# Eight-head attention layers: softmax sums done in one go in a bank of the shared ring, their accumulator's bank used as a third score bank

## What is computed

```
xn  = group_norm(x) * gn_w + gn_b
qkv = qkv_w @ xn + qkv_b                      # per head: q, k, v of 32 x 1024
w   = softmax(einsum('bct,bcs->bts', q * scale, k * scale))
a   = einsum('bts,bcs->bct', w, v)
out = (xn or x) + proj_w @ a + proj_b         # xn in layer 2, x in layer 3
```

## Time and profile before

| | us |
|---|---|
| median of 3 runs | 1897.23 |
| the profiled execution | 1903.71 |
| its span, first to last instruction | 1901.6 |

### The profile page before, as it was taken

The page is one execution under the profiler, slowest core; times in us unless marked ns, Lnnn a source line. Parts: engine busy times, 40 slices in busy tenths (PEclk is TensorE's granted clock), DMA queues, the critical chain, the costliest instruction groups (busy, mean ns, idle before and its releaser), DMA issues.

```text
span 1901.6 us, 24881 instructions
## 1 busy us (share of the span) xinstructions
PE 1707.0 (90%) x8222; PEld 1007.7 (53%) x8222; DVE 1099.5 (58%) x1571; ACT 928.7 (49%) x1487; POOL 1010.4 (53%) x402
## 2 busy tenths in 40 slices
PE   3887959999992899999999998999999999999987
PEld 2666748888882454454444444445444444454422
DVE  2545535454432856765766667666675576666712
ACT  2433414343322165655565564565665656555553
POOL 2322312122103166775787585767776578757764
PEclk7989979999996698999999998999999999999988
DMA  3000000000001222021130230202202112032000
GB/s 137 17 17 17 1 1 1 1 1 1 1 1 32 56 68 67 1 68 45 25 67 1 67 84 1 67 20 54 67 2 67 42 49 67 2 90 68 1 23 22
DMA packets 24989, 67.44 MB, mean 35 GB/s; under 512 B 7200, under 2 KB 8992, under 8 KB 24864
## 3 DMA queue, kind: packets, MB, share of 16 engines
q1 hardware_dynamic: 24864, 65.78, 14.3%
HBM read 7.82 MB, written 4.19 MB: 6 GB/s over the span
## 4 chain that ended last, share of the span: by engine, by line
PE 50%; DVE 9%; issue 3%; ACT 3%; POOL 1%; DMA 1%; SPq 1%; DVEq 0%; POOLq 0%; ACTq 0%
PE psO L869 13%; PE psA L950 12%; PE psD L925 11%; PE psD L79 10%; DVE A L979 5%; PE psO L872 4%; DVE BNS L998 4%; ACT PR L1121 2%; POOL PA L1187 1%; DMA QS<-MROW 1%; SPq L1207 0%; ACT XH L1065 0%; SPq L1209 0%; DVE A L981 0%; DMA QS<-SL 0%
## 5 line engine op out<-in xcount | busy, mean ns | idle before, releaser
L1121 ACT ACTIVATE PR<-psA 128x512 f32<-128x512 f32 x1024 | 585.0, 597 | 520.3 <-PE psA L950 491.3
L998 DVE TENSOR_REDUCE BNS<-psD 128x1 f32<-128x512 f32 x1024 | 632.6, 685 | 241.5 <-PE psD L925 241.4
L1187 POOL TENSOR_TENSOR PA<-PA,PR 128x2048 f32<-128x2048 f32 x128 | 585.1, 4571 | 20.5 <-ACT PR L1121 9.3
L950 PE MATMUL psA<-QS,KS 97*128 97x512 f32 x1024 | 463.5, 461 | 39.1 <-ACT PR L1121 30.5
L925 PE MATMUL psD<-KS,QS 96*128 96x512 f32 x1024 | 419.2, 446 | 33.2 <-DVE BNS L998 17.8
L950 PEld LDWEIGHTS psA<-QS,KS 97*128 97x128 f32 x1024 | 194.2, 193 | 335.0 <-ACT PR L1121 180.0
L869 PE MATMUL psO<-PR,V 128*32 128x512 f32 x2048 | 273.3, 642 | 0.7 <-ACT PR L1121 0.7
L925 PEld LDWEIGHTS psD<-KS,QS 96*128 96x128 f32 x1024 | 204.2, 200 | 123.9 <-DVE BNS L998 80.2
L594 POOL TENSOR_SCALAR P<-P,RS 128x1024 f32<-128x1024 f32 x64 | 71.8, 1122 | 356.1 <-DVE RS L345 356.1
L1187 POOL TENSOR_TENSOR PA<-PR 128x2048 f32<-128x2048 f32 x32 | 146.0, 4564 | 134.9 <-ACT PR L1121 134.9
L979 DVE RECIPROCAL A<-psO 128x512 f32<-128x512 f32 x32 | 107.4, 3358 | 148.0 <-PE psO L872 148.0
(11 more groups left out here) (129 smaller groups left out, 1810.7 us busy)
## 6 DMA issues: line engine op xcount, KB each, us to landing
KS<-SH SPq DMA_DIRECT2D x128, 128.0 KB, 2.5
QS<-SH SPq DMA_DIRECT2D x128, 128.0 KB, 2.5
KS<-SL SPq DMA_DIRECT2D x64, 128.0 KB, 2.5
QS<-SL SPq DMA_DIRECT2D x64, 128.0 KB, 2.5
X<-x SPq DMA_DIRECT2D x4, 1024.0 KB, 7.6
out<-X SPq DMA_DIRECT2D x4, 1024.0 KB, 4.4
KH<-KL SPq DMA_DIRECT2D x8, 128.0 KB, 2.3
QH<-KL SPq DMA_DIRECT2D x8, 128.0 KB, 2.4
```

What stands on the lines that cost most here:

```text
L950: e.matmul(psA[:, s % 2, :], KS[0:STACK + 1, p, q, j * PART:(j + 1) * PART], QS[0:STACK + 1, p, q, h * HALF:(h + 1) * HALF], start=True, s ...
L998: top = e.tensor_reduce(MXH[:, h, q, tile:tile + 1], full, AX.X, ALU.max)
L1121: e.activation(PR[:, J % 4, (s % QUADH) * HALF:(s % QUADH + 1) * HALF], psA[:, s % 2, :], ACT.Exp, scale=scale).then_inc(exp_done, 1)
L1187: e.tensor_tensor(PA[:, :], PR[:, (J - 1) % 4, :] if j == 1 else PA[:, :], PR[:, J % 4, :], ALU.add).then_inc(sum_done, 1)
```

## The change

`psO` bank 1 no longer holds the sums. It becomes a third bank for scores (`score_bank`), and score s waits for exp s-3 instead of s-2; only scores 0 and 1 of a phase with P even still wait for s-2. The three sum pieces of a half are a new side unit "z" in the ring of `psD`: `sums` does sum 7, sum 6 and pa one after the other, at 34.9 (step 35) for half 0 and at 2.9 (step 3) of the next phase for half 1. DVE's `take_half` is z's taker: its reciprocal reads the ring's bank and then frees it. av 6 and 7 are both issued at step 33 of the half (so those of half 1 at step 1 of the next phase; before, av 6 was at step 62). The m units begin at 6.5 instead of 5.5, the hole for the reciprocal is 35 to 38.5 in all phases (before 35 to 39, and one more at 12 to 13.5 in phases with P even). `av_done` counts 7 pieces a half instead of 8, and the waits on it follow. POOL's first add of a half waits for z instead of pa. In `tail` the last z and the output projection use ring banks in turn.

```diff
-        M_AT = (5.5, 58)
-        HOLES = [[(35, 39)], [(12, 13.5), (35, 39)]]
+        M_AT = (6.5, 58)
+        HOLES = [(35, 38.5)]
...
+                     "z": (34.9, 2.9)}
         BANKS = 4
+        SCORE_BANKS = 3
...
+        def score_bank(s, p):
+
+            i = (s + p) % SCORE_BANKS
+            return psA[:, i, :] if i < 2 else psO[:, 1, :]
...
-        WEIGH = [("av", 0, 13), ("av", 1, 13), ("av", 2, 18), ("av", 3, 18), ("av", 4, 26), ("av", 5, 26),
-                 ("av", 6, 30), ("sum", 6, 30), ("av", 7, 34), ("sum", 7, 34), ("pa", NT, 35)]
...
+        WEIGH = [(0, 13), (1, 13), (2, 18), (3, 18), (4, 26), (5, 26), (6, 33), (7, 33)]
+        PIECES = NT - 1
+
+        def weighed(P, J):
+
+            h, j = J // NT, J % NT
+            return PIECES * 2 * P + PIECES * h + min(j + 1, PIECES)
...
+                    def sums(full, P, h):
+
+                        for j in (NT - 1, NT - 2, NT):
+                            if j == NT:
+                                wait(e, sum_done, ADDS * (2 * P + h + 1))
+                            source = PA[:, :] if j == NT else PR[:, j % 4, :]
+                            source = source.rearrange("p (q n) -> p q n", q=QUADH)
+                            for q in range(QUADH):
+                                mm = e.matmul(full[CH * q:CH * q + CH, :], ones[:, 0:CH], source[:, q, :],
+                                              start=(j == NT - 1), stop=(j == NT))
+                            if j == NT - 2:
+                                mm.then_inc(av_done, 1)
+                        return mm
...
+                        elif u == "z":
+                            mm = sums(full, P - i, i)
...
-                            wait(e, exp_done, STEPS * P + s - 1)
-                            e.matmul(psA[:, s % 2, :], KS[0:STACK + 1, p, q, j * PART:(j + 1) * PART],
+                            wait(e, exp_done, STEPS * P + s - (1 if p == 0 and s < 2 else SCORE_BANKS - 1))
+                            e.matmul(score_bank(s, p), KS[0:STACK + 1, p, q, j * PART:(j + 1) * PART],
...
-                        for i in range(2 * CT):
-                            e.wait_ge(vec_free, TAIL["vector"] - BANKS + 1 + i)
-                            output(bank(4, i), i, 2 * NGRP, 3).then_inc(d_full, 1)
+                        e.wait_ge(vec_free, TAIL["vector"] + 1)
+                        sums(bank(4, 2), NGRP - 1, 1).then_inc(d_full, 1)
+                        for i in range(2 * CT):
+                            e.wait_ge(vec_free, TAIL["vector"] + max(i, 2))
+                            output(bank(4, 3 + i), i, 2 * NGRP, 3).then_inc(d_full, 1)
...
-                    def take_half(P, p, h):
-
-                        wait(e, av_done, (2 * P + h + 1) * NT)
+                    def take_half(full, p, h):
+
                         out_ap = A[:, p, h * HALF:(h + 1) * HALF]
-                        e.reciprocal(out_ap, psO[:, 1, :])
+                        e.reciprocal(out_ap, full).then_inc(vec_free, 1)
                         e.drain()
                         e.tensor_tensor(out_ap, psO[:, 0, :], out_ap, ALU.mult).then_inc(out_done, 1)
```

More of the change, by code:

```diff
@@ L698, in side_units @@
             units = [(u, at, i) for u, ats in halves.items() for i, at in enumerate(ats)]
+            if first:
+                units = [x for x in units if x[0] != "z" or g == 1 and x[2] == 0]
             n = QUADH * NT * 2
-            spacing = (M_AT[1] - M_AT[0] - sum(b - a for a, b in HOLES[g])) / n
+            spacing = (M_AT[1] - M_AT[0] - sum(b - a for a, b in HOLES)) / n
             for i in range(n):
                 at = M_AT[0] + i * spacing
-                for a, b in HOLES[g]:
+                for a, b in HOLES:
                     at += (b - a) * (at > a)
@@ L726, in attention_stack @@
         assert LOOP["all"] % BANKS == 0
-        assert all("".join(x[0] for x in u[-BANKS:]) == "m" * (BANKS - 1) + "T" for u in UNITS)
+        assert all("".join(x[0] for x in u[-BANKS:]) == "m" * (BANKS - 1) + "T" for u in UNITS[:4])
         def base_of(kind, place, r):
+            if place == 4:
+                return TAIL[kind]
             return BASE[kind][place] if r is None else r * LOOP[kind] + BASE[kind][place]
@@ L988, in add_residual, with take @@
                                                       in1=xb, op0=ALU.add, op1=ALU.add)
-                    def take(place, r, k, G, g, proj, layers):
+                    def take(place, r, k, p, G, g, proj, layers):
                         u, _, i = UNITS[place][k]
@@ L1020, in phase @@
                     def phase(P, p, G, g, place, r, layers, proj=None, norm=None, norm_b=None):
-                        events = [(at, 0, k, "unit") for k, (u, at, i) in enumerate([] if G is None else UNITS[place])
+                        events = [(at, 0, k, "unit") for k, (u, at, i) in enumerate(UNITS[place])
                                   if u not in "vwkqKQ"]
@@ L1026, in phase @@
                             events.append((XN_AT + 0.1, 0, 0, "weights"))
-                        if P is not None:
-                            if not (isinstance(P, int) and P == 0):
-                                events.append((TAKE_AT - HALF_STEPS, 0, 1, "half before"))
-                            events.append((TAKE_AT, 0, 0, "half"))
                         for _, _, k, what in sorted(events):
-                            if what == "half before":
-                                take_half(P - 1, 1 - p, 1)
-                            elif what == "half":
-                                take_half(P, p, 0)
-                            elif what == "weights":
+                            if what == "weights":
                                 split_next_weights()
@@ L1090, in phase @@
                         events = []
-                        for k, (u, at, i) in enumerate([] if G is None else UNITS[place]):
+                        for k, (u, at, i) in enumerate(UNITS[place]):
                             if u in "vwkqKQ":
@@ L1182, in phase @@
                                 wait(e, exp_done, STEPS * P + QUADH * (J + 1))
-                                if j == 1:
-                                    wait(e, av_done, NT * (2 * P + h))
-                                else:
+                                if j == 1 and not (isinstance(P, int) and P == h == 0):
+                                    before = [k for k, (u, _, i) in enumerate(UNITS[place]) if u == "z" and i == 1 - h][0]
+                                    e.wait_ge(d_full, base_of("all", place, r) + before + 1)
+                                if j > 1:
                                     wait(e, sum_done, ADDS * (2 * P + h) + j - 1)
```

67 lines of the change are left out of this document (29 added, 38 removed).

## The result

| | before | after |
|---|---|---|
| median of 20 runs each, us | 1901.47 (1895.06 to 1905.62) | 1908.15 (1900.86 to 1915.53) |
| ratio of the runs, 95% interval | | 1.0035 (1.0021 to 1.0048) |
| the profiled execution, us | 1903.71 | 1915.53 |
| its span | 1901.6 | 1913.4 |
| mean granted clock | 0.932 | 0.926 |

The changed kernel is 6.7 us slower where 1.7 us faster was forecast; both are within the 0.5% called no change, but the interval excludes 1. The forecast of 1895.5 us started from 1897.2, a median of 3 runs; 20 runs put the kernel before at 1901.5, so 4.2 us of the distance to 1908.15 are that start and 8.4 the change. The profiled execution of after is the slowest of its 20, the one of before is 2.2 us above its median.

What follows compares the result with a forecast made beforehand. No engine was full: DVE set steps 4 to 28 (P odd) and step 36 to T, PE mostly the rest. Terms 10.2 - 5.6 - 4.9 - 4.9 + 6.0 - 2.5 = -1.7 gave 1895.5 us from 1897.2, range 1886 to 1906.

Steps and rivals of the forecast that it cites:

- full-speed terms: The forecast's changes by stage and for the last phase, with no term for the clock; sum -1.7 us.
- D: Stretch from T (a phase's last marked event) through score 0 to the next step 4; forecast +10.2 us in all.
- plain boundaries: Written-out or plain phase boundaries, nine of them; forecast +0.68 us each, +6.1 in all.
- saving of 0.2 for a run: Entering and leaving a run of pieces on PE costs 0.2 us; one run fewer saves that.
- A: Step 4 to 28, set by DVE where P is odd; forecast -5.6 us for seven odd phases, -4.9 for seven even.
- B: Step 28 to 36, bound by PE; one run of pieces fewer, forecast -4.9 us in all.
- C: Step 36's reciprocal to T, set by DVE; one more reduce, shorter pause: +0.4 us a phase, +6.0 in fifteen.
- jumps back: Three loop jumps where score 0 waits 2.23 us for PE's instructions; moving pieces neutral, -0.2 each, -0.6 in all.
- gated boundaries: Three boundaries inside the hardware loop where score 0 already waits for the row; forecast 1.56 us each, +4.7.
- Rival 2: Half speed comes at the phase boundary behind T, 1.7 us each, 25 in fifteen, 1921 us; chance 0.20.
- Rival 3: The forecast itself: scores wait less for exps, m units more for DVE; 1886 to 1906 us, chance 0.45.
- last phase: Last phase and tail: -3.3 us from three banks, +0.8 for av 6 in the tail; -2.5, bounds -6 to +1.

Runs made afterwards that it cites:

- e6: Kernel before with two idle matmuls at each of steps 5 to 8, beside the reciprocal: 1886.30 us, ratio to before 0.9927.
- e4: Changed kernel with two idle matmuls behind each of scores 61 to 63 and 36 to 39: 1877.13 us, ratio to before 0.9866.
- e1: Changed kernel with its third score bank taken away, two banks left: 1908.38 us, ratio to before 1.0037.
- e7: Changed kernel with idle matmuls behind scores 61 to 63 and 36 to 39, but two score banks: 1893.55 us, ratio to before 0.9958.
- e5: Changed kernel with z ahead of av 6 and av 7, which follow beside the reciprocal; only the multiply waits for them: 1851.24 us, ratio to before 0.9747.
- e3: Changed kernel with two idle matmuls behind each of scores 61 to 63, in the wait for the row: 1899.28 us, ratio to before 0.9983.

## Why the prediction failed, by its own steps

- **The full-speed terms.** Their sum held. D: score 0 stands 2.73 to 2.94 behind T (2.85 forecast), at the plain boundaries. The stretch after it grew by 1.83, not 1.56; the saving of 0.2 for a run wasn't seen. A where P is odd: 23.12 to 22.42, -0.7 (-0.8 forecast); even 29.4 to 28.7, -0.7 (-0.7). B -0.3 and -0.56 (-0.2 and -0.44). C 21.35 to 21.84, +0.5 (+0.4). For the 13 phases these steps gave D +8.9, A -9.8, B -4.0, C +5.2: +0.3 in all, and the runs show +10.2, -9.6, -5.6, +5.9: +0.9. Within D that is luck in part: the seven plain boundaries cost 6.6 (4.8 forecast), the three gated ones 1.0 (4.7), and the three jumps back some 2.6 (-0.6). The forecast took the wait at a jump back as a fixed delay from T. In after score 0 comes only 0.6 to 0.9 us sooner there than before, and not 1.76, and the pieces follow it.
- **The gated boundaries** inside the hardware loop: +4.7 forecast for three. In after the row lands 2.1 to 2.2 us after its issue everywhere, where it took 3.4 to 3.6 there before; score 0 comes at 2.93 to 3.03 and not at 4.3 to 4.5, so they gain 1.3 to 1.4 each before they pay 1.7 to 1.8. The term was mis-sized by 3.7 us. Why it landed late before is open.
- **The clock, A.** The forecast left the half speed of the earlier trace rows where it was, and called the 2.01 us of DVE's idle time behind it structural; 1.3 of them are half speed (0.72 at full clock, in e6). This half speed went in all 13 phases, which is worth 21.3 us. That wasn't among the terms at all, and so A where P is odd came to 22.4 and not to the 23.6 given as a sign.
- **The clock, C and D: the step that failed.** The sum has no term for the clock; it stood at nothing, and the profiled execution shows +14.7 us in the 13 phases (A -21.3, C +22.7, D +13.3). Rival 2 was set aside with "around step 36 PE is as sparse, and there it is 1.00". The row was right and the inference wrong: it told of the kernel before, and the change makes just that stretch sparser. Pieces that stood between scores go before the reciprocal, z holds a ring bank through it, three scores go at once. The prediction had written down each of these three edits, for DVE's sake, and didn't ask what they do to PE's waits. Half speed came to C in 12 phases that had none before, at 1.5 us where 3.4 us of it were granted and 2.4 to 2.6 where 6.8 were, and to the boundary in 8, at 1.4 to 2.8 each. That 14 idle matmuls a phase took nearly all of it away, and 31 us with it (e4), shows what it cost. By the rule of the Trainium skill cited in the prediction ("TensorE: Matmul & The Clock Gate", HAM oscillation — how this bites in real kernels), waits between bursts bring the clock down; the trace agrees at both places, though in P = 8 and at the boundary behind it no wait is over 1.22 us, which is shorter than the DMA waits of the page's case. The section behind it ("A second HAM failure mode: psum-queue depth-cycling"), on a kernel that cycles through PSUM banks, describes short but frequent idle times between groups of matmuls as enough; P = 8 and P = 9 above show that nearly the same short waits (0.22 to 0.65 us) may or may not be.
- **Rival 2's price**, 1.7 a boundary and 1921 in all: right in size for one fall (3.4 us of half speed on pure PE work cost 1.6: 8.79 to 10.37 in e1). Its sign, a granted clock below 1.00 between T and z, came in 8 of 14 boundaries and not in all 15. It had no C and left out what A gives back; as those two nearly cancel, the 13.3 us at the boundary, the place it named, are most of the net.
- **Rival 3, a gain that nobody collects.** Its sum is right: e1 and after are alike. Its reason is half right. In A and C the bank is worth 0.1 to 0.4 at full clock, as said. But e7 shows 16 us in all (17 by the ratios), of which the forecast had the last phase and not the 2.5 of P = 0, and half speed gives it back: e1 has it in C in 4 phases, after in 13.
- **The last phase**: -2.5 forecast, -6.1 measured, at the bound given. Both of its terms were mis-sized, in opposite directions. The part with scores took 63.62 us before and 50.65 in after, -13.0 and not -3.3; what follows it took 22.3 and now takes 29.2, +6.9 and not +0.8, since the last sums wait for POOL's adds, which end at 1892.8, 8.6 us behind the start of the last score. The bank alone is 4.8 in all (e7 to e4). Before, 17.1 us of half speed lay in the part with scores (0.87 in the earlier trace rows), in after none, and that wasn't counted.

## What to carry to other kernels

Where an engine other than PE sets a stage's pace, PE's idle time is free only as long as the clock holds: for each stretch that a change makes sparser, price the half speed as if it came, and look at which work follows it (the two av pieces behind such a gap took 3.64 us instead of 1.92). When work is moved, don't move it from a wait to a dense place; put it into the wait: with the same pieces e5 is 51 us below the kernel before, and after 7 above it. A buffer's worth is no number of its own: this bank was worth 0, 16 and 37 us (0, 17 and 33 by the ratios) in three orders of the same work.

## What was not expected of the hardware

- 14 added matmuls a phase, that compute nothing, gained 31 us (1908.15 to 1877.13), and 8 gained 14 to 16 in the kernel before (ratio 0.9927, 1902.28 to 1886.30); the granted clock rose with them (0.926 to 0.949, and 0.932 to 0.938).
- The same program at the same place gets half speed in one phase and not in the next (C of P = 8 and 9). Much of the spread of a kernel's runs goes with it: executions of after at a mean granted clock of 0.932 took 1900.9 to 1903.4 us, at 0.928 1907 to 1910, at 0.925 1912.6. The start of P = 0, behind the same code, lies between 665.1 and 672.6 us in the profiled executions of the twelve kernels. A single profile of this kernel can't decide a few us.
- Half speed removed at one place appears at others: in e6 C and D got what A had lost, in e3 C kept 12 of 13 and A got it in three phases.
